# A new order of the same work on every engine of a ViT block kernel, with more quarter products side by side

## What is computed

```python
t = unfold3x3(x)                                   # [16, 3136, 576]
h1 = relu(t @ W1 + b1)                             # 64 wide
s = sigmoid(h1 @ W2 + b2)                          # 576 wide
h = (t * s) @ W3 + b3                              # 64 wide
h = concat([cls_tok, h], axis=1)                   # 3137 tokens
# attention on u = layernorm(h), then rmsnorm with w_norm1
q, k, v = split(rmsnorm(u) @ w_qkv); q, k = elu(q) + 1, elu(k) + 1     # 8 heads of 8
kv = sum_n k[n] v[n]; z = 1 / (q . sum_n k[n] + eps)
a = u + (q kv z) @ w_out + b_out
h = h + a + rmsnorm(a)
# six experts, two chosen for each token
f = layernorm(h)
gates = softmax of the top 2 of softmax(relu(f @ rw1 + rb1) @ rw2 + rb2)
e = relu(relu(f @ ew1 + eb1) @ ew2 + eb2) @ ew3 + eb3     # for each expert
out = h + sum of gate * e over the two chosen
```

## Time and profile before

| | |
|---|---|
| median of 3 runs | 2068.82 us |
| lowest and highest | 2064.14 and 2079.31 us |
| profiled execution | 2064.24 us, span 2062.5 us |
| TensorE busy (share of the span) | 1929.0 us (94%) |
| VectorE busy | 1295.1 us (63%) |
| ScalarE busy | 1086.0 us (53%) |
| GpSimd busy | 499.9 us (24%) |
| DMA | 168.31 MB, 82 GB/s on the mean |

### The profile page before, as it was taken

The page is one execution under the profiler, slowest core; times in us unless marked ns, Lnnn a source line. Parts: engine busy times, 40 slices in busy tenths (PEclk is TensorE's granted clock), DMA queues, the critical chain, the costliest instruction groups (busy, mean ns, idle before and its releaser), DMA issues.

```text
span 2062.5 us, 38206 instructions
## 1 busy us (share of the span) xinstructions
PE 1929.0 (94%) x13033; PEld 809.1 (39%) x13033; DVE 1295.1 (63%) x3687; ACT 1086.0 (53%) x2213; POOL 499.9 (24%) x346
## 2 busy tenths in 40 slices
PE   7888999999999999999999999999999999977775
PEld 2333344434444443444444444444444434333332
DVE  3455667576767676766667666767576767654553
ACT  3443555555555555555565655555555555543333
POOL 0112222222222222222222222222222222222120
PEclk9999999999999999999999999999999999978887
DMA  3121242424242423333333424242424232223222
GB/s 114 69 77 51 54 110 59 115 58 115 58 115 65 108 84 89 89 85 95 78 101 72 108 65 112 61 115 58 115 60 114 74 99 73 49 64 64 59 50 61
DMA packets 77184, 168.31 MB, mean 82 GB/s; under 512 B 6048, under 2 KB 62272, under 8 KB 76992
## 3 DMA queue, kind: packets, MB, share of 16 engines
q1 hardware_dynamic: 76992, 165.87, 31.0%
HBM read 151.80 MB, written 14.05 MB: 80 GB/s over the span
## 4 chain that ended last, share of the span: by engine, by line
issue 70%; POOL 19%; PE 8%; ACT 1%; DMA 1%; DVE 1%; POOLq 0%; SPq 0%; ACTq 0%; DVEq 0%
POOL rstd_b L877 4%; POOL rms_b L877 4%; POOL rstd_h L877 4%; POOL sum_b L899 3%; POOL h L915 3%; PE ps L352 2%; PE ps L324 2%; PE ps L368 1%; PE ps L386 0%; ACT th L701 0%; DMA gate_sp<-gates_d 0%; PE ps L371 0%; PE ps L400 0%; PE ps L443 0%; PE ps L631 0%
## 5 line engine op out<-in xcount | busy, mean ns | idle before, releaser
L701 ACT ACTIVATE th<-ps,b_half 128x448 f32<-128x448 f32 x504 | 300.5, 635 | 294.8 <-PE ps L352 247.3
L941 DVE SCALAR_TENSOR_TENSOR gated<-th,x_tile 128x448 f32<-128x448 f32 x504 | 307.6, 621 | 63.8 <-ACT th L701 37.7
L352 PE MATMUL ps<-h,packed 64*128 64x448 f32 x896 | 226.9, 582 | 30.9 <-ACT f L830 16.3
L1270 DVE TENSOR_TENSOR gh<-f,gate_sp 128x448 f32<-128x448 f32 (+1 forms) x342 | 190.6, 612 | 101.1 <-DMA gate_sp<-gates_d 88.5
L820 ACT ACTIVATE f<-ps,packed 128x448 f32<-128x448 f32 (+1 forms) x342 | 196.4, 627 | 107.5 <-PE ps L594 107.5
L830 ACT ACTIVATE f<-ps,packed 128x448 f32<-128x448 f32 (+1 forms) x342 | 201.6, 634 | 84.0 <-DVE gh L1270 82.8
L368 PE MATMUL ps<-gated,w_half 128*64 128x448 f32 x896 | 207.0, 562 | 0.0
L877 POOL TENSOR_TENSOR rstd_u<-var_u,exponent 112x8 f32<-112x8 f32 (+1 forms) x57 | 92.3, 1619 | 468.9 <-DVE var_u L967 468.9
L324 PE MATMUL ps<-x_tile,packed 128*64 128x448 f32 x896 | 185.2, 555 | 8.6 <-DMA x_tile<-x_rows 7.0
L594 PE MATMUL ps<-y,packed 64*128 64x448 f32 (+1 forms) x684 | 182.1, 610 | 2.9 <-ACT f L820 2.4
L946 DVE TENSOR_REDUCE sums_c<-ps 112x8 f32<-112x512 f32 (+1 forms) x57 | 39.0, 684 | 225.6 <-PE ps L379 225.6
(11 more groups left out here) (140 smaller groups left out, 3036.5 us busy)
## 6 DMA issues: line engine op xcount, KB each, us to landing
gate_sp<-gates_d SPq DMA_DIRECT2D x112, 672.0 KB, 7.6
x_tile<-x_rows SPq DMA_DIRECT2D x56, 696.0 KB, 5.4
x_tile<-x_rows SPq DMA_DIRECT2D x56, 580.0 KB, 3.9
out<-out_t SPq DMA_DIRECT2D x56, 224.0 KB, 5.2
gates_d<-gates_c SPq DMA_DIRECT2D x56, 21.0 KB
packed<-pack SPq DMA_DIRECT2D x1, 682.0 KB, 9.3
packed<-pack SPq DMA_DIRECT2D x1, 448.0 KB, 5.9
packed<-pack SPq DMA_DIRECT2D x1, 366.0 KB, 3.0
```

The lines of the kernel that those rows point to most:

```text
L352: pe.matmul(bank(S0 + img), cst("w2", m * P, (m + 1) * P)[half(img)], h1[half(img), :], start=True, stop=True).then_inc(s_done, 1)
L701: act.activation(th[(u + s) % 4][:, :], bank(S0 + u % 2), ACT.Tanh, bias=b2_half[:, m:m + 1], scale=0.5).then_inc(th_set, 1)
L941: dve.scalar_tensor_tensor(as_rows(gated[u % 4][:, :]), as_rows(th[(u + s) % 4][:, :]), 1.0, x_view(s, u), ALU.add, ALU.mult).then_inc(gat ...
L1270: dve.tensor_tensor(gh[j % 4][:, 0:n], f2[j % 4][:, 0:n], gate_sp[:, j % 2 * (E // 2) + j // 2, 0:n], ALU.mult).then_inc(gh_set, 1)
```

## The change

The loops over steps on all five engines are put in a new order, and steps run from 0 to 68 instead of 1 to 76. No operation is added or left out (the one line taken out of gates_part never issued anything). On TensorE q_prod now follows w2(4), and w3(4) follows out_proj; stage a's products and the first part of stage b are done one step earlier relative to the loop's number, w1(0) to w1(3) one step ahead. Two waits are exchanged with it, since another reader now comes last in a bank. GpSimd's loop is renumbered and rms_b comes before sum_b. SyncE's queue changes from save, store, spread, load to load, spread, save, store.

```diff
-        STEPS = range(1, LAST_STEP + 1)
+        STEPS = range(0, LAST_STEP + 1)
 (SyncE)
-                if 1 <= step - 10 <= CLS_T: save_gates(step - 10)
-                if 1 <= step - 12 <= CLS_T: store_out(step - 12)
-                if 1 <= step - 10 <= CLS_T: spread_gates(step - 10)
                 if 3 <= step + 2 <= BLOCKS: load_x(step + 2)
+                if 1 <= step - 8 <= CLS_T: spread_gates(step - 8)
+                if 1 <= step - 7 <= CLS_T: save_gates(step - 7)
+                if 1 <= step - 10 <= CLS_T: store_out(step - 10)
 (spread_hn on TensorE)
                 pe.wait_ge(rxh_set, r + 1)
-                pe.wait_ge(qf_set, r + 1)
+                if 1 <= r - 8:
+                    pe.wait_ge(f1_set, E * (r - 8 - 1) + 2)
+                else:
+                    pe.wait_ge(qf_set, r + 1)
 (expert_h1 on TensorE)
-                        pe.wait_ge(kvsum_set, f + 8 + 1)
+                        pe.wait_ge(qf_set, f + 8 + 1)
...
                 if ep == 1:
                     pe.wait_ge(f1_set, E * (f - 1) + 2)
+                    if f + 8 <= BLOCKS:
+                        pe.wait_ge(kvsum_set, f + 8 + 1)
 (TensorE's loop, the new one)
+                if 1 <= step - 9 <= CLS_T: var_mean_b(step - 9)
+                if 1 <= step <= BLOCKS: w1(step, 4)
+                if 0 <= step - 1 <= BLOCKS: center_a(step - 1)
+                if 1 <= step - 10 <= CLS_T: expert_h2(step - 10, 2); expert_out(step - 10, 0); expert_out(step - 10, 1)
+                if 1 <= step <= BLOCKS: w2(step, 0)
+                if 0 <= step - 1 <= BLOCKS: var_mean_a(step - 1)
+                if 1 <= step - 9 <= CLS_T: spread_c(step - 9)
+                if 1 <= step - 10 <= CLS_T: expert_out(step - 10, 2)
+                if 1 <= step <= BLOCKS: w2(step, 1)
+                if 1 <= step - 9 <= CLS_T: router(step - 9)
+                if 1 <= step - 8 <= BLOCKS: att_channels(step - 8)
+                if 1 <= step - 9 <= CLS_T: logits(step - 9)
+                if 1 <= step <= BLOCKS: w2(step, 2); w3(step, 0)
+                if 0 <= step - 1 <= BLOCKS: spread_u(step - 1)
+                if 1 <= step <= BLOCKS: w2(step, 3)
+                if 0 <= step - 1 <= BLOCKS: kv_prod(step - 1)
+                if 1 <= step <= BLOCKS: w3(step, 1); w2(step, 4)
+                if 0 <= step - 1 <= BLOCKS: q_prod(step - 1)
+                if 1 <= step <= BLOCKS: w3(step, 2); w3(step, 3)
+                if 1 <= step - 8 <= CLS_T: out_proj(step - 8)
+                if 1 <= step <= BLOCKS: w3(step, 4)
+                if 1 <= step - 9 <= CLS_T: gates_channels(step - 9); expert_h1(step - 9, 0)
+                if 1 <= step - 8 <= CLS_T: mean_sq_b(step - 8)
+                if 1 <= step - 10 <= CLS_T: out_tokens(step - 10)
+                if 0 <= step - 1 <= BLOCKS: spread_hn(step - 1)
+                if 1 <= step - 9 <= CLS_T: expert_h2(step - 9, 0)
+                if 0 <= step - 1 <= BLOCKS: kv_outer(step - 1)
+                if 1 <= step - 9 <= CLS_T: expert_bias(step - 9); expert_h1(step - 9, 1)
+                if 1 <= step - 8 <= CLS_T: spread_b(step - 8)
+                if 1 <= step - 7 <= BLOCKS: attention(step - 7)
+                if 1 <= step - 9 <= CLS_T: expert_h1(step - 9, 2); expert_h2(step - 9, 1)
+                if 1 <= step - 8 <= CLS_T: center_b(step - 8)
+                if 1 <= step + 1 <= BLOCKS: w1(step + 1, 0); w1(step + 1, 1); w1(step + 1, 2); w1(step + 1, 3)
 (ScalarE's loop, first part of the new one)
+                if 0 <= step - 2 <= BLOCKS: copy_v(step - 2, 0)
+                if 1 <= step - 1 <= BLOCKS: gate_tanh(step - 1, 8)
+                if 0 <= step - 2 <= BLOCKS: exp_q(step - 2)
+                if 1 <= step - 1 <= BLOCKS: unfold_out(step - 1)
+                if 1 <= step - 10 <= CLS_T: gates_copy(step - 10)
+                if 0 <= step - 2 <= BLOCKS: copy_v(step - 2, 1)
+                if 1 <= step - 9 <= CLS_T: square_b(step - 9)
+                if 1 <= step - 10 <= CLS_T: relu1(step - 10, 0); relu1(step - 10, 1)
+                if 1 <= step - 11 <= CLS_T: out_copy(step - 11)
+                if 1 <= step - 10 <= CLS_T: relu2(step - 10, 0); relu1(step - 10, 2); relu1(step - 10, 3)
+                if 1 <= step - 10 <= CLS_T: relu2(step - 10, 1); relu1(step - 10, 4); relu1(step - 10, 5)
+                if 1 <= step - 9 <= CLS_T: center_b(step - 9); square_c(step - 9)
+                if 1 <= step - 10 <= CLS_T: relu2(step - 10, 2); relu2(step - 10, 3)
+                if 1 <= step <= BLOCKS: hidden(step)
+                if 1 <= step - 10 <= CLS_T: relu2(step - 10, 4); relu2(step - 10, 5)
+                if 0 <= step - 1 <= BLOCKS: center_a(step - 1); square_a(step - 1)
+                if 1 <= step <= BLOCKS: gate_tanh(step, 0); gate_tanh(step, 1); gate_tanh(step, 2)
+                if 1 <= step - 9 <= CLS_T: router_relu(step - 9)
+                if 1 <= step <= BLOCKS: gate_tanh(step, 3); gate_tanh(step, 4); gate_tanh(step, 5)
 (VectorE's loop, the part of the new one that the text speaks of)
+                if 1 <= step - 1 <= BLOCKS: gate_pixels(step - 1, 7)
+                if 1 <= step - 10 <= CLS_T: gates_part(step - 10, 8)
+                if 1 <= step - 1 <= BLOCKS: gate_pixels(step - 1, 8)
+                if 1 <= step - 10 <= CLS_T: gates_part(step - 10, 9)
+                if 0 <= step - 2 <= BLOCKS: elu_q_min(step - 2)
+                if 1 <= step - 10 <= CLS_T: gates_part(step - 10, 10)
+                if 0 <= step - 2 <= BLOCKS: elu_q(step - 2); elu_k_min(step - 2)
+                if 1 <= step - 9 <= CLS_T: residual(step - 9)
+                if 0 <= step - 2 <= BLOCKS: spread_hn(step - 2); elu_k(step - 2, 0); elu_k(step - 2, 1)
+                if 1 <= step - 9 <= CLS_T: mean_sq_b(step - 9)
+                if 0 <= step - 2 <= BLOCKS: normed_hn(step - 2); sum_kv(step - 2)
...
+                if 1 <= step - 10 <= CLS_T: gate_hidden(step - 10, 0); gate_hidden(step - 10, 1)
+                if 1 <= step - 9 <= CLS_T: variance_b(step - 9)
+                if 1 <= step - 10 <= CLS_T: gate_hidden(step - 10, 2); gate_hidden(step - 10, 3)
+                if 1 <= step - 10 <= CLS_T: gate_hidden(step - 10, 4)
```

More of the change, by code:

```diff
@@ L27 @@
 CLS_T = BLOCKS + 1
-LAST_STEP = 76
+LAST_STEP = 68
 SLOTS = 10
@@ L652, in _ @@
             for step in STEPS:
[L653 to L667, removed]
@@ L846, in _ @@
             for step in STEPS:
-                if 1 <= step - 10 <= CLS_T: relu1(step - 10, 4); relu1(step - 10, 5); relu2(step - 10, 2)
-                if 1 <= step - 10 <= CLS_T: relu2(step - 10, 3)
+                if 0 <= step - 2 <= BLOCKS: copy_v(step - 2, 0)
[3 more added lines that the diff above has]
+                if 1 <= step - 10 <= CLS_T: gates_copy(step - 10)
@@ L866, in _ @@
-                if 1 <= step - 9 <= CLS_T: gates_copy(step - 9)
-                if 1 <= step <= BLOCKS: unfold_out(step)
-                if 1 <= step - 10 <= CLS_T: out_copy(step - 10)
-                if 1 <= step - 9 <= CLS_T: relu1(step - 9, 0); relu1(step - 9, 1); relu1(step - 9, 2)
-                if 1 <= step - 9 <= CLS_T: relu1(step - 9, 3); relu2(step - 9, 0); relu2(step - 9, 1)
-                if 1 <= step - 8 <= CLS_T: center_b(step - 8); square_c(step - 8)
+                if 1 <= step - 9 <= CLS_T: gate_top(step - 9)
@@ L1289, in _ @@
             for step in STEPS:
-                if 0 <= step - 2 <= BLOCKS: sum_kv(step - 2)
+                if 1 <= step - 1 <= BLOCKS: gate_pixels(step - 1, 0); gate_pixels(step - 1, 1)
+                if 1 <= step - 1 <= BLOCKS: gate_pixels(step - 1, 2)
+                if 1 <= step - 10 <= CLS_T: gates_part(step - 10, 0)
+                if 0 <= step - 2 <= BLOCKS: spread_u(step - 2)
+                if 1 <= step - 10 <= CLS_T: gates_part(step - 10, 1)
+                if 1 <= step - 1 <= BLOCKS: gate_pixels(step - 1, 3)
@@ new lines, in _ @@
+                if 1 <= step - 10 <= CLS_T: gates_part(step - 10, 2)
+                if 0 <= step - 2 <= BLOCKS: normed_u(step - 2)
+                if 1 <= step - 10 <= CLS_T: gates_part(step - 10, 3); gates_part(step - 10, 4)
+                if 1 <= step - 1 <= BLOCKS: gate_pixels(step - 1, 4)
+                if 1 <= step - 10 <= CLS_T: gates_part(step - 10, 5)
+                if 1 <= step - 1 <= BLOCKS: gate_pixels(step - 1, 5)
+                if 1 <= step - 10 <= CLS_T: gates_part(step - 10, 6)
@@ new lines, in _ @@
+                if 1 <= step - 1 <= BLOCKS: gate_pixels(step - 1, 6)
+                if 1 <= step - 10 <= CLS_T: gates_part(step - 10, 7)
+                if 1 <= step - 1 <= BLOCKS: gate_pixels(step - 1, 7)
[4 more added lines that the diff above has]
+                if 1 <= step - 10 <= CLS_T: gates_part(step - 10, 10)
@@ L1301, in _ @@
+                if 1 <= step - 10 <= CLS_T: result(step - 10)
                 if 0 <= step - 1 <= BLOCKS: scales_a(step - 1)
-                if 1 <= step - 9 <= CLS_T: normed_b(step - 9)
```

(12 more changed lines are left out.)

62 lines of the change are left out of this document (14 added, 48 removed).

## The result

The changed kernel takes 2097.18 us (median of 5 runs, 2094.60 to 2102.89) against 2068.82 for the kernel before (2063.36 to 2079.60): ratio 1.0131, 95% interval 1.0087 to 1.0175. It is slower by 1.3%. The forecast was 2030 with a range up to 2075, so the time lies outside the range and on the other side.

The account below looks back on a forecast made before the run. TensorE's list bounded the kernel before; afterwards the gates loop (33.2 us) over the list (32.65). 46 x (33.77 - 33.2) = 26 us plus drain 9 from 2064.24 gives 2029, stated as 2030; range 1968 to 2075.

Parts of the forecast that it names:

- The transfer, save to gate_hidden: SyncE's save and spread until VectorE's first gate_hidden: 13.8 us, bounds 10.8 and 14.26.
- From out(1) to the next save: Loop's TensorE part: 13.6 us of products and 0.4 of waits to out_proj/w3(4), then 2.2 to the save.
- the floor of 31.5: TensorE's list per step: 33.77 less 1.80 for two product pairs and 0.5 idle gives 31.5 us.
- (a): On TensorE, expert_h1(0) must wait until unfold_out has read bank L0; cost 0.45 us a step.
- (b): On TensorE, mean_sq_b and the transposes wait for square_b on ScalarE; cost 0.3 us a step.
- (c): On TensorE, logits waits for the router's ReLU, with only att_channels between; cost 0.25 us a step.
- (d): w3(3) and w3(4) wait for gate_pixels 7 and 8 on packed VectorE; cost 0.15 us, bounds 0 and 0.6.
- (e): ScalarE's out_copy waits 0.8 us for an earlier store to land; TensorE loses nothing.
- The rival that made the kernel slower: Store landing late holds ScalarE at out_copy and delays the spread: period 34.9, some 2115 us; chance 0.06.
- the last rival: TensorE's quarters don't run side by side, 1.80 us returns to the list: period 34.4, about 2090 us; chance 0.03.
- The list alone binds: Transfer finishes early and TensorE's list sets the period: 31.6 to 32.7 us, 1955 to 2005 us; chance 0.27.
- Ends: Fill steps: nothing, +-5 us in all; drain: some 9 steps, 1 us less each, bounds 0 and 2.

Follow-up runs that it names:

- e1: Changed kernel with SyncE's queue reordered: x load ahead of the save, then save, spread, store; 2028.51 us, 0.9824 of the kernel before.
- e2: Changed kernel with store_out alone moved behind the spread, x load staying ahead of it; 2040.43 us, 0.9876 of the kernel before.
- e4: Changed kernel with scales_a on VectorE put directly behind deviations_a, ahead of normed_b and result; 2066.91 us, 1.0026 of the kernel before.
- e6: Changed kernel with both e1's queue order and e4's early scales_a; 2004.11 us, 0.9687 of the kernel before.

## Why the prediction was wrong

The mechanism that I named as the likeliest is the one that binds: the loop through save, spread, gate_hidden, out(1) and the next gates. e1 and e2 show it by opening it. What failed is the size of two of its terms, by 0.73 and 0.83 us.

- **The transfer, save to gate_hidden: 13.8 taken, 14.53 measured.** It lies above my upper bound too, 14.26. The bound was the transfer of the kernel before, taken as the worst because no traffic is added: save, store and x go ahead of the spread in both. What the bound left out is when they start. Before, the x load was issued 0.94 us ahead of the save (1004.57 against 1005.50), so part of its bytes moved before my clock ran; in the new order it is issued 0.85 behind the save, with the store in between. From the x load's issue to gate_hidden the time did fall, from 15.2 to 13.7 us, but the load's later start took more than that back. "The save's own way to memory no longer comes on top" was right, and the spread is issued 3 us earlier, but behind bytes that have not landed: 12.65 us from its issue to gate_hidden, where I bounded with 9.30. e2 gives the store's share, 1.27 us; I had used the store to fill today's 4.96 and given it no price of its own.
- **From out(1) to the next save: 14.0 + 2.2 = 16.2 taken, 17.03 measured.** Some 0.5 of the 0.83 is rstd_u at 3.08 us: 17.03 becomes 16.44 in e4, and 16.88 in e1 becomes 16.39 in e6. I had left scales_a at its old length and put no wait on it. Between 0.1 and 0.2 is the pairs at 0.91 and 0.93 instead of 0.80. 0.13 is the three steps at half clock; e1 and e2, which have none between 400 and 1700 us, stand at 16.88 and 16.90.
- **From gate_hidden to out(1):** 3.2 taken, 3.14 measured.
- **TensorE's list: the floor of 31.5.** e1 gives 32.06, e6 31.8. Of these 0.3 to 0.6, 0.19 is the pairs (1.61 instead of 1.80). The rest may be changes of tile form, which I had costed at nothing, ±0.2; that part isn't shown.
- **New waits.** (a) expert_h1 for unfold_out, 0.45: 0.39. (b) mean_sq_b, 0.3: 0.08. (c) logits, 0.25: 0.06. (d) w3, 0.15: none. In their place came 0.29 at kv_prod, on u_a behind rstd_u, and 0.14 at the transposes to channels, neither of them on my list.
- **(e) out_copy** for the store: 0.8 taken, 1.0 measured, and absorbed as said. The rival that made the kernel slower named the store, which e2 shows to cost 1.2 us of the step, but by the wrong way: it landed 2.4 us after its issue and held ScalarE as forecast, and cost time by its bytes ahead of the spread's. The landing above 5 us that it asked for did not come, the period above 33.8 did.
- **The quarters run side by side,** against the last rival. **The list alone binds** is e1's and e6's state, not this kernel's.
- **Ends.** Drain: 1 us less each was taken; the gate transposes stand at 1905.12 and 1930.92, 25.80 apart instead of 27.37, and the whole gives 6.6 instead of 9. Fill: nothing, ±5, was taken, and it costs 7; that copy_v stands behind unfold_out is argued, not shown.

Two sums of the rivals are off: 2085 us for a period of 34.1 and 2115 for 34.9 leave out the 9 us of the drain that the forecast counts. By the forecast's own sum they are 2070 and 2107.

Against the 2029 us that were forecast for the profiled execution, 2100.44 is 71 too much: 44 x (34.57 - 33.2) = 60 of the full steps, 7.0 of the fill and 2.4 of the drain make 69 of it. The loop was forecast above the list, so each microsecond missed on it counted whole, and up to 2075 the range had room for only 1.0 a step.

## What to carry to other kernels

- When an order is changed on every engine, write down the DMA queue's order of before and after first, with the bytes of each entry, and for each transfer on a loop sum the bytes that are issued ahead of it and have not landed when it is issued. The queue's order alone does not tell: here save, store and x went ahead of the spread before and after. An independent load or store goes where it has nothing urgent behind it: moving the store alone was worth 57 us here, load and store together 69, more than the whole rearrangement.
- Price a step as the larger of TensorE's list and each loop through other engines, and on the loop cost the small instructions too: a 112x8 operation on GpSimd grew by 1.45 us, and some 0.5 of it was on the loop.
- Where products of one form stand alone among others, look for a partner in the other two quarters: a pair saved 0.8 us each time, as long as its readers kept their distance.
